# Window mask of the attention layers: from TensorE products to ScalarE copies into the score banks

## The reference

```python
q, k, v = split(shift_tokens(x) @ Wqkv)           # 16 heads of 64
q = l2norm(q) * q_scale; k = l2norm(k) * k_scale  # then a rotary turn of both
# windows of 32 queries see the 32 keys before them and their own 32
mask = (it < jb) | (it > jb + 32) | (jb == -1)
sim = where(mask, -max, einsum(bq, bk2) * 8)
out = einsum(softmax(sim), bv2) @ Wo + x
```

## Time and profile before

| what | value |
| --- | --- |
| median of 3 runs | 5136.06 us (5130.78 to 5147.4) |
| profiled execution, its own time | 5136.26 us |
| its span | 5134.4 us |
| mean granted TensorE clock | 0.954 of full |
| busy: TensorE, VectorE, GpSimd, ScalarE | 4374.8, 3356.9, 2570.1, 2441.1 us |
| share of the span: TensorE, VectorE, GpSimd, ScalarE | 85%, 65%, 50%, 48% |

### The profile page before, as it was taken

One profiled execution on the slowest core, in us unless ns is written; L12 is line 12 of the kernel. 1 busy time (PEld: TensorE's weight loads), 2 busy tenths in 40 slices (PEclk: granted clock), 3 DMA queues, 4 the chain that ended last, 5 costly groups with the idle time before them and its releaser, 6 DMA issues. The chain is left out here.

```text
span 5134.4 us, 182125 instructions
## 1 busy us (share of the span) xinstructions
PE 4374.8 (85%) x70227; PEld 2980.5 (58%) x70227; DVE 3356.9 (65%) x7024; ACT 2441.1 (48%) x5161; POOL 2570.1 (50%) x4541
## 2 busy tenths in 40 slices
PE   8999946765899888998889988999889998899985
PEld 6777733653566545666456664666546665466653
DVE  3555533365777657776577765777667776677765
ACT  3555543222555535554355543555435554355542
POOL 0000000001777627776277762777627776277761
PEclk9999968887999999999999999999989999899998
DMA  1000001201111111111111111111111111011111
GB/s 37 5 4 4 2 1 50 58 6 48 32 32 32 25 30 32 32 32 25 30 32 32 32 25 30 32 32 32 26 29 32 32 32 30 25 32 32 32 24 33
DMA packets 76107, 143.17 MB, mean 28 GB/s; under 512 B 19654, under 2 KB 57748, under 8 KB 68116
## 3 DMA queue, kind: packets, MB, share of 16 engines
q1 hardware_dynamic: 75284, 131.92, 10.5%
HBM read 35.40 MB, written 4.19 MB: 8 GB/s over the span
## 5 line engine op out<-in xcount | busy, mean ns | idle before, releaser
L2437 DVE TENSOR_TENSOR n_tt<-n_pp,n_rot 128x1024 f32<-128x1024 f32 x768 | 922.2, 1220 | 615.7 <-ACT n_sq L2307 615.5
L1939 POOL TENSOR_TENSOR n_pre<-n_tt 128x512 f32<-128x512 f32 x768 | 964.1, 1278 | 288.6 <-DVE n_tt L2437 288.2
L2055 PE MATMUL n_pp<-n_wqkv,n_xT 128*128 128x512 f32 x1536 | 794.9, 620 | 10.6 <-ACT n_xT L2302 10.4
L1974 POOL TENSOR_TENSOR n_pre<-n_pre,n_rn 128x512 f32<-128x512 f32 x768 | 777.6, 1045 | 34.2 <-POOL n_rn L1962 34.2
L2307 ACT ACTIVATE n_sq<-n_pp 128x512 f32<-128x512 f32 x768 | 459.3, 598 | 596.8 <-PE n_pp L2055 595.2
L2444 DVE TENSOR_REDUCE n_ss<-n_sq 128x8 f32<-128x512 f32 x768 | 518.5, 675 | 0.0
L2329 ACT ACTIVATE n_E<-n_E 128x512 f32<-128x512 f32 x384 | 235.7, 630 | 582.1 <-DVE n_E L2456 582.1
L2072 PE MATMUL n_pp<-ident,n_pre 128*128 128x128 f32 x3072 | 417.5, 278 | 51.3 <-POOL n_pre L1974 50.6
L2072 PEld LDWEIGHTS n_pp<-ident,n_pre 128*128 128x128 f32 x3072 | 359.2, 144 | 172.1 <-issue 93.5
L2318 ACT COPY n_qkT<-n_pp 128x512 f32<-128x512 f32 x768 | 421.5, 603 | 61.7 <-PE n_pp L2072 60.1
L2086 PE MATMUL n_pp<-n_wo,n_OT 128*128 128x128 f32 x3072 | 403.3, 285 | 8.8 <-ACT n_OT L2324 4.9
(11 more groups left out here) (263 smaller groups left out, 8240.9 us busy)
## 6 DMA issues: line engine op xcount, KB each, us to landing
n_Vx<-n_V SPq DMA_DIRECT2D x192, 256.0 KB, 3.9
n_Vx<-n_V SPq DMA_DIRECT2D x192, 192.0 KB, 3.6
n_wqkv<-in_L_ffn_Wqkv SPq DMA_DIRECT2D x6, 1536.0 KB, 6.5
e_w<-in_L_ffn_w SPq DMA_DIRECT2D x32, 256.0 KB, 3.0
m_Y<-e_ye SPq DMA_DIRECT2D x64, 64.0 KB, 2.0
n_wo<-in_L_ffn_Wo SPq DMA_DIRECT2D x6, 512.0 KB, 7.3
a_xs<-in_L_attn_x SPq DMA_DIRECT2D x16, 128.0 KB, 2.1
x_kept<-X SPq DMA_DIRECT2D x1, 2048.0 KB, 8.3
```

The lines of the kernel that those rows point to most:

```text
L1939: nc.gpsimd.tensor_tensor(d, s[0], s[1][:, :, ::-1, :], ALU.add).then_inc(s_add, 1)
L1974: nc.gpsimd.tensor_tensor(d, d, bcast(rn[:, j, t, 8 * half:8 * half + 8], 2, D), ALU.mult).then_inc(s_kn, 1)
L2055: nc.tensor.matmul(pp[:, c % 2, :], xT[:, j * P:(j + 1) * P], wqkv[:, t * I + 512 * half:t * I + 512 * half + 512], start=True, stop=True) ...
L2437: nc.vector.tensor_tensor(tt[:, c % 4, :, :].rearrange("p s (h d) -> p s h d", d=D), bcast(pp[:, c % 2, :].rearrange("p (h d) -> p h d", d ...
```

## The change

The two bf16 products that wrote the mask go, with `masks`, the identity `eye` and the bf16 copy of the mask, which VectorE made once. The mask is kept in fp32. ScalarE now copies it into the two banks of pS (`lay_mask`), and the score products are added to what the copies wrote. The copies for the other half stand right behind `copy_weights`, ahead of the `copy_qk`; the ones for the first half of a layer stand at the head of ScalarE's prologue, behind a wait for the feed-forward's last sum. On TensorE the scores wait for the mask (`s_mask`) and for the copies of q and k, and there are one or two `held` more in a half. At the start two fp32 products write both banks once. Uncut in all that is spoken of:

```diff
-        win_f = sb("win_f", [P, 2, 2 * W])
-        win = sb("win", [P, 2, 2 * W], BF16)
-        eye = sb("eye", [P, P], BF16)
+        win = sb("win", [P, 2, 2 * W])
...
-            def masks(N, j):
-
-                after(pe, s_sub, 4 * N + 2 * j)
-                for e in range(2):
-                    nc.tensor.matmul(pS[:, e, :].rearrange("p (i s) -> p i s", s=2 * W), eye[:, :],
-                                     bcast(win[:, j, :], 1, 8), start=True, stop=False, skip_group_check=True)
-
...
-                    if not nxt:
-                        after(pe, s_qkT, 8 * N + 4 * j + 4)
-                    masks(N, j)
                     if j == 1:
+                        held(pe, s_held)
                         weigh(u, 0)
                     elif prev:
+                        held(pe, s_held)
                         weigh(1 - u, 1)
                     if nxt:
                         project_qk(N + 1, 4 * j)
                         project_qk(N + 1, 4 * j + 1)
-                        after(pe, s_qkT, 8 * N + 4 * j + 4)
                         project_v(N + 1, 2 * j, bank("v", 2 * j, 1))
                         project_v(N + 1, 2 * j + 1, bank("v", 2 * j + 1, 1))
+                    after(pe, s_mask, 4 * N + 2 * j + 2)
+                    after(pe, s_qkT, 8 * N + 4 * j + 4)
+                    held(pe, s_held)
                     scores(j)
...
             pe.wait_ge(s_clear, 3)
-            pe.wait_ge(s_cast, 2)
+            for e in range(2):
+                nc.tensor.matmul(pS[:, e, :].rearrange("p (t c) -> p t c", c=C), ident[:, :], X[:, 0:4, :],
+                                 start=True, stop=True).then_inc(s_wipe, 1)
...
             act.wait_ge(s_clear, 3)
+            act.wait_ge(s_c, 16 * 3)
+            act.wait_ge(s_wipe, 2)
...
+            def lay_mask(N, j):
+                after(act, s_sub, 4 * N + 2 * j)
+                for e in range(2):
+                    nc.scalar.copy(pS[:, e, :].rearrange("p (i s) -> p i s", s=2 * W), bcast(win[:, j, :], 1, 8)
+                                   ).then_inc(s_mask, 1)
+
             def prologue(N, l):
+                after(act, f_y, NG * l)
+                lay_mask(N, 0)
...
                     copy_weights(N, j, 0)
                     copy_weights(N, j, 1)
+                    if j == 0:
+                        lay_mask(N, 1)
+                    elif nxt:
+                        lay_mask(N + 1, 0)
                     if nxt or not j:
                         copy_qk(N + j, 4 - 4 * j, bank("turn", 4 - 4 * j, j))
...
-            nc.vector.tensor_copy(win[:, :, :], win_f[:, :, :]).then_inc(s_cast, 1)
-            nc.vector.tensor_copy(eye[:, :], ident[:, :]).then_inc(s_cast, 1)
```

More of the change, by code:

```diff
@@ L1788, in l1_network @@
         s_c = sem("constants_loaded", False)
-        s_cast = sem("constants_cast", False)
         s_wa = sem("attention_weights_loaded", False)
@@ L1809, in l1_network @@
         s_qkT = sem("qkT_copied")
+        s_wipe = sem("score_banks_written", False)
+        s_mask = sem("mask_laid")
         s_S = sem("scored")
@@ L1881, in _ @@
                              ).then_inc(s_c, 16)
-            sp.dma_start(win_f[:, :, :], consts["window"]).then_inc(s_c, 16)
+            sp.dma_start(win[:, :, :], consts["window"]).then_inc(s_c, 16)
             with sp.Fori(0, LAYERS) as l:
```

## The result

| what | before | after |
| --- | --- | --- |
| median | 5134.97 us (4 runs) | 5233.38 us (4 runs, 5229.91 to 5233.9) |
| ratio, with its 95% interval | | 1.0186 (1.0168 to 1.0204) |
| span of the profiled execution | 5134.4 us | 5232.1 us |
| mean granted TensorE clock | 0.954 | 0.953 |
| busy: TensorE, ScalarE | 4374.8, 2441.1 us | 4353.8, 2618.8 us |

The change costs 98 us, where +49 was forecast: the sign and the mechanism held, the size was at half.

The account below looks back on a forecast made before the run. TensorE and ScalarE in lockstep at a half's end were taken as the bound: 174 x 0.39 = +68 us, first halves -3, last halves -6, issue gaps -10, together +49 on 5136, giving 5185 us; range 5148 to 5240.

Parts of the forecast that it names:

- What bounds the kernel: End of an attention half: TensorE and ScalarE run in lockstep with little slack; ScalarE's idle time lies elsewhere.
- The saving, 0.42 in a half: TensorE ahead of `weigh`: removing the pair of mask products saves 0.42 us a half, at most 81 us.
- Price of the pair, D = 1.00: ScalarE's queue: the two mask copies of a half take D = 1.00 us, two of the usual spacings.
- Slack of the copies, "D - 0.61": Copies ahead of `copy_qk`: a half changes by D - 0.61, from 0.19 us slack and 0.42 of masks; +68 us.
- Gaps of issue, -10: Before `weigh`: 51.3 us of gaps put down to issue; a later `weigh` may find its instructions there, -10 us.
- Ends of layers, -9: First halves of layers keep the masks' cost, -3 us; last halves no longer hold masks and `weigh`, -6 us.
- Who else could be late: Other engines: VectorE still waits for the scores with 0.20 us left; GpSimd covered; `copy_x` covered by less than 0.1.
- The clock stayed: Rival, TensorE: more idle time makes its clock fall, up to 30 us more, 5215 us; chance 0.03.
- The copies did not fit in: Rival: copies lie wholly in ScalarE's idle time, halves keep all of 0.42 us; 5057 us, faster, chance 0.10.
- The gaps of issue did not close: Rival: issue gaps before `weigh` close and D = 0.92; 5146 to 5154 us, chance 0.06 within 0.3%, 0.01 just above.
- The dear pair at D = 1.26: Rival: dearer copies, or VectorE takes over; a half grows by 0.65 us; 5240 us, chance 0.16.
- a faster write to PSUM: ScalarE's mask copies: writing PSUM might be faster, allowing under 0.30 us a copy, below which the time falls.

Follow-up runs that it names:

- the late copies: The changed kernel with the mask copies moved to the end of a half, behind the last square, where ScalarE is idle; 5077.99 us, ratio 0.9885.
- both kernels that have it there: The changed kernel, 5233.38 us, and the kernel before with two extra ScalarE mask copies into spare SBUF at the same place, 5306.54 us.
- the run with one copy: The changed kernel with one mask copy in each half instead of two, the second score bank getting no mask; 5139.43 us, ratio 0.9999.
- the run with the cover: The changed kernel with mask copies at the end of a half, plus two bf16 products ahead of `weigh`, which overwrites them; 5119.24 us, ratio 0.9974.
- the `held` alone: The kernel before, mask products kept, with a `held` added ahead of `weigh` and of the scores; 5125.47 us, ratio 0.9986.
- the run with the copies one step later: The changed kernel with the mask copies behind the first two `copy_qk` and ahead of the square; 5181.8 us, ratio 1.0099.

## Why the prediction was right in kind and short in size

- **What bounds the kernel.** Right. The place in ScalarE's queue decides: the same work 61 us faster at one place and 98 us slower at another.
- **The saving, 0.42 in a half.** Right in the usual halves: 0.43 and 0.38 with the late copies.
- **Price of the pair, D = 1.00.** Measured 1.04, in both kernels that have it there. That is what the Trainium skill gives ("ScalarE: Activation LUTs", "What ACT_TABLE_LOAD costs", an estimate of 0.52 us each); the page was right where I went by the nearest rows. Worth 0.04 x 174 = 7 us.
- **Slack of the copies, "D - 0.61".** This term was mis-sized. The third `turn_qk` started at 1436.39, 0.80 late against 1434.73 + 0.86, and from its start to the projection there were 0.98 us instead of 0.87: each of the two groups of four is released just before it starts, so its first weight load is not ahead, and 0.16 us pass from its first to its second product instead of 0.11. The projection came 0.91 late where I had 0.82 for D = 1.00. Less 0.42, and with 0.06 for the second `turn_qk`, that is within 0.02 of the 0.53 that a half 0 grew. In all a half changes by D - 0.51, as the run with one copy bears out (15.45 and 16.25 us at D = 0.52). With D that is 0.53 instead of 0.39: 92 us instead of 68, 24 of the missing 49.
- **Gaps of issue, -10.** Wrong in sign; this step failed. I took it that a later `weigh` would find its instructions there. What the longer halves have over the usual grew by 13 us. The run with the cover shows the reason as far as it goes: the mask products themselves had been hiding such time, and with them gone some of their 0.42 us is not saved. That is 23 us against the forecast. What the hidden time is stays open.
- **Ends of layers, -9.** All that lies outside the 174 halves gave 7 us together, 2 from the forecast. That is luck as much as insight: the same part gave 13 us with the `held` alone, where the masks still wait as in the earlier trace rows, and 22 to 25 us in the kernels with the copies later. I didn't separate these by a run.
- **Who else could be late.** VectorE had its 0.2 us left and still waited for the scores, as worked out; in the run with the copies one step later it was the bound. GpSimd's last norm ended at 1436.1, ahead of the fourth transposes; covered. But I looked at the last norm alone: its second one now releases the second `turn_qk` of a usual half 0, which costs 0.06 us there. The clock stayed, 0.953 for 0.954. `copy_x` did no visible harm.
- **Rivals.** The copies did not fit in; that rival's point of decision, D = 0.61, is measured at about 0.5, one copy. The gaps of issue did not close. The dear pair at D = 1.26 named 5240 us, near the time, for the wrong reason: the copies weren't that dear. And it was that price which set the top of the range, so that 5233 us lies inside it is partly luck.

## What to carry to other kernels

When work moves to an engine with idle time, look where in its queue the idle time lies, and what stands behind the new instruction: here 1.04 us ahead of copies that free banks cost 0.95 us in each half, and the same 1.04 us ahead of an idle stretch cost nothing in a usual half. Follow each result of the delayed stretch (here the banks, and the square with VectorE and GpSimd behind it), since easing one chain uncovers the next. And an engine's work that ends just before a stretch of many small instructions may be hiding a delay in it, so count its removal at less than its length.

## What the runs showed of the hardware

- ScalarE's copy of 128x512 from SBUF takes the same place in its queue into PSUM as into SBUF: 1.04 us a pair in either case. I had kept a faster write to PSUM as a possibility; the Trainium skill ("ScalarE: Activation LUTs", "Step-by-step: what each stage is for") calls PSUM the faster port for ScalarE's results, and here no difference shows in the distance of starts. The records differ by 0.03 us a pair, 1.13 for 1.16.
- Eight transposes whose two groups of four are each released just before they start take 0.98 us, start to start, where those that flow take 0.87. A weight load came 0.12 us behind the end of the copy or norm that released it (1436.76 to 1436.88, 1434.12 to 1434.24).
- A `held` on TensorE's queue (51 ns in its record) adds nothing to a usual half, neither in the kernel before nor doubled in the changed one; doubled, the whole was 17 us slower in the median. Part of that stays open.
- The halves with more than the usual time stand at the same places of the instruction list in all six layers, and the places differ between kernels with different TensorE queues.
